# The order of the steps of a four-layer transformer kernel, written out step by step

## The chip, the cores and the metric

The kernel runs on one core of one Trainium2 chip. The metric is the device time of one execution in microseconds (us). Five queues of instructions run side by side: TensorE (PE; its weight loads are shown apart as PEld), VectorE (DVE), ScalarE (ACT), GpSimd (POOL) and SyncE (SP), which here issues all DMAs.

## What is computed

A batch of 4 items of 512 tokens by 256 channels goes through four blocks, all in float32:

```python
# layer 0: one head of 256; rmsnorm and film, q/k/v, softmax, projection, rmsnorm and film, MLP 256-1024-256
attn = softmax(einsum('bnd,bmd->bnm', Q, K) * D ** -0.5); x = x + (attn @ V @ proj_w + proj_b)
# layer 1: 16 heads of 16, modulated layernorm, q and k normalised to length one, gated residuals
q = l2norm(q) * exp(min(scale_mul, log 100)); k = l2norm(k); o = softmax(q @ k.T) @ v
# layer 2: 16 heads of 16, modulated layernorm, scale 16 ** -0.5, gated residuals
# layer 3: 16 heads of 16, attention and projection, then a modulated layernorm; no MLP
```

## The kernel before

**Work.** A job is one item in one layer: job j has layer j // 4 and item j % 4, 16 jobs in all. Jobs 0 to 3 have one head. Jobs 4 to 15 have 16 heads, in 4 units of 4 heads; unit u belongs to job u // 4. Most matrix products split each float32 operand in a high and a low part and add three products (`product`, lines 602 to 604).

**Steps.** The program is a list of 2446 steps, `PLAN`, each a triple (kind, job or unit or layer, index). Every engine walks through the whole list and issues its own part of each step, so the list alone sets the order on each of the five queues; between the queues there are semaphores, and each wait names the step that it waits for. Kinds that the text speaks of:

- `scores` (line 701): 16 steps a unit, one 64-row matmul each, for one head (n = i % 4) and one block of 128 keys; ScalarE then takes the exponential into `probs` (line 908, or line 905 for two neighbouring banks at once in layer 1).
- `max` (line 676): 16 steps a unit in layers 2 and 3, a 63-row matmul of the scores the other way round; VectorE reduces each to row maxima (line 1231). `shift` (line 693) transposes a unit's maxima, VectorE copies them to `cT` (line 1238), and SyncE writes them as the last row of the stack `SQ` (line 570) that `scores` of that unit read. In layer 1 a bound (`gmax`, line 684; `shift1`, line 689; `crow`, line 560) takes its place.
- `av` (line 714): the product of `probs` and the values, 4 steps a unit; the last is copied out by ScalarE.
- `hT1`, `hT2`, `q`, `k`, `v`, `qktok`, `oT1`, `oT2`, `proj`, `fc1`, `gelu`, `fc2a`, `fc2`: transposes, projections and MLP of a job. `gelu` is a step of ScalarE and GpSimd alone (lines 968 and 1334); `fc1`'s banks are read there. `stat1`, `norm1`, `stat2`, `norm2` are the layer norms. `modrow` and `mod` (lines 626 and 631) make a layer's modulation. `scores0`, `soft0`, `pT0` are the attention of layer 0.
- `load_*`, `split_*`: a piece of weights is loaded into one buffer and split into high and low part; a load waits until the piece before it is split. `stack`: six DMAs that build the stacks of one unit's q and k.

**Banks.** All matmuls but `av` write to one of `RING` = 7 banks, which are handed out in turn over the list (`USES`); `claim` makes TensorE wait until the step seven uses before it has been read:

```python
                n = USE[(kind, a, i)]
                if n >= RING:
                    k, b, m = USES[n - RING]
```

Scores and maxima of heads with even and odd n lie in different halves of the array's rows (`r = BLK * (n % 2)`). In layer 1 `double` finds the pairs of scores whose banks are neighbours:

```python
            return bounded(unit_job(a)) and USE[(kind, a, i - i % 2 + 1)] == first + 1 and first % RING < RING - 1
```

**The order before.** Each kind has a table of times in ticks (16 ticks a job), for the first jobs one table each, for the others one a layer; `multi_window` goes through a job in pairs of ticks, and a pattern such as "p6 A p8 0 p4 1" says how the 16 scores and maxima of a pair of ticks (p), the two `av` steps (A) and the remaining steps of each tick (0, 1) follow each other.

Of the kernel before, what the change touches and what calls it, by code (L numbers as in the profile page):

```python
# [61 lines left out]

SINGLE0 = {"stat1": (-16.2,), "norm1": (-23.7,), "hT1": (-15.4, -14.74), "q": (-11.01, -9.91), "k": (-5.2, -3.95),
           "v": (2.61, 5.47), "scores0": (-0.85, -0.65, 1.31, 3.06), "soft0": (1.31, 1.96, 4.26, 4.92),
           "pT0": (6.87, 7.42, 7.68, 9.03), "proj": (10.18, 10.73), "stat2": (13.99,),
           "norm2": (14.84,), "bias": (-3.15,)}
SINGLE1 = {"stat1": (-19.05,), "norm1": (-4.8,), "hT1": (-9.18, -8.83), "q": (-6.12, -4.01), "k": (-6.57, -5.31),
           "v": (2.6, 3.92), "scores0": (-1.64, -1.29, 1.78, 2.88), "soft0": (2.49, 2.84, 3.36, 3.71),
           "pT0": (7.11, 7.47, 7.82, 8.68), "proj": (11.73, 12.09), "stat2": (13.82,),
           "norm2": (14.33,), "bias": (-5.4,)}  # L70
SINGLE2 = {"stat1": (-16.5,), "norm1": (-14.55,), "hT1": (-9.7, -9.49), "q": (-6.76, -3.06), "k": (-5.65, -3.6),
           "v": (3.0, 4.07), "scores0": (-0.14, 0.81, 1.78, 4.23), "soft0": (2.59, 4.44, 5.01, 5.51),
           "pT0": (7.92, 8.38, 8.63, 8.99), "proj": (12.74, 12.9), "stat2": (16.24,),
           "norm2": (16.64,), "bias": (-0.3,)}
FFN0 = {"hT2": (16.72, 17.27), "fc1": (20.32, 20.68, 21.03, 21.44, 24.73, 25.09, 26.87, 27.22), "gelu": (21.79, 27.58),
        "fc2a": (24.96, 26.06), "fc2": (30.07, 32.88)}
# [1416 lines left out]
```

## Time and profile before

| | before |
|---|---|
| median of 3 runs | 1159.32 us (1157.16 to 1162.14) |
| profiled execution, its own time | 1158.51 us |
| its span, first to last instruction | 1156.7 us |
| mean granted TensorE clock | 0.985 of full speed |
| busy: PE, PEld, DVE, ACT, POOL | 94%, 61%, 61%, 69%, 42% of the span |

Times in the rows are from the start of the span. Layer 0 has TensorE to itself until about 225 us; the scores of layer 1 begin at 225.1 us, those of layer 2 at 550.6 us, those of layer 3 at 885.2 us. "A <- B" with a time is the time that A's engine sat idle until B released it. Matmuls are pipelined: a row's duration reaches past the start of the next, so the distance of starts is the rate.

### The profile page before, as it was taken

What the parts mean: (1) busy time and instruction counts of PE and PEld (TensorE: products, weight loads), DVE (VectorE), ACT (ScalarE), POOL (GpSimd) and SP (SyncE); (2) the same over time, 40 slices, a digit from 0 to 9 for tenths busy, and PEclk for the clock granted to TensorE, in tenths of its full rate; (3) what the DMA queues carried; (4) which work ended last, traced back from release to release, by engine and by line L of the source; (5) the groups of instructions that cost most, each with busy time, mean ns of one, the idle gap of its engine ahead of it and who ended that gap; (6) DMA issues with size and microseconds to landing.
All of it is one profiled execution on the core that took longest, in us unless ns stands there. A gap on an engine that the chain in (4) does not pass through costs nothing.

```text
span 1156.7 us, 19632 instructions
## 1 busy us (share of the span) xinstructions
PE 1085.3 (94%) x6697; PEld 706.0 (61%) x6697; DVE 702.5 (61%) x1479; ACT 794.0 (69%) x1331; POOL 490.3 (42%) x446
## 2 busy tenths in 40 slices
PE   8799989789899999999999999999999999999985
PEld 5577878555565656656657566666656566555442
DVE  6554446545264364234864865865865856898974
ACT  3563655477888678796686686687686787686763
POOL 2553642613633633654335453244344345254122
PEclk9999999999999999999999999999999999999998
DMA  7000001213303203221132231032121211232301
GB/s 234 18 29 28 1 20 38 52 31 101 88 28 95 54 2 90 75 64 29 28 84 65 69 102 38 2 83 65 41 71 29 52 42 52 55 84 56 84 12 36
DMA packets 36385, 64.45 MB, mean 56 GB/s; under 512 B 7208, under 2 KB 22312, under 8 KB 36288
## 3 DMA queue, kind: packets, MB, share of 16 engines
q1 hardware_dynamic: 36288, 63.20, 20.6%
q8 instruction: 56, 0.92, 0.3%
q14 instruction: 41, 0.34, 0.1%
HBM read 22.90 MB, written 2.12 MB: 22 GB/s over the span
## 4 chain that ended last, share of the span: by engine, by line
PE 72%; DVE 9%; ACT 8%; issue 5%; POOL 4%; DMA 1%; SPq 0%; POOLq 0%; DVEq 0%; ACTq 0%
PE AVB L714 13%; PE rings L602 13%; PE rings L604 11%; PE rings L603 11%; PE rings L701 10%; PE rings L676 6%; DVE m L1231 2%; ACT probs L908 2%; PE rings L754 2%; PE rings L749 2%; PE rings L645 2%; POOL gT_l L1334 1%; ACT L908 1%; PE rings L766 1%; POOL tok L1355 1%
## 5 line engine op out<-in xcount | busy, mean ns | idle before, releaser
L1231 DVE TENSOR_REDUCE m<-rings 128x1 fp32r<-128x512 f32 x512 | 319.1, 682 | 101.6 <-PE rings L676 78.4
L908 ACT ACTIVATE probs<-rings 128x512 f32<-128x512 f32 x570 | 297.3, 617 | 96.0 <-PE rings L676 84.5
L701 PE MATMUL rings<-SQ,SK 64*128 64x512 f32 x768 | 236.3, 440 | 12.5 <-ACT probs L905 4.7
L676 PE MATMUL rings<-SK,SQ 63*128 63x512 f32 x512 | 200.9, 459 | 5.4 <-ACT probs L908 4.2
L714 PE MATMUL AVB<-probs,V 128*32 128x512 f32 x1536 | 192.9, 609 | 0.6 <-issue 0.4
L701 PEld LDWEIGHTS rings<-SQ,SK 64*128 64x128 f32 x768 | 107.9, 185 | 139.1 <-issue 52.6
L1334 POOL TENSOR_TENSOR gT_l<-gT_f,gT_h 128x512 fp32r<-128x512 f32 x96 | 121.1, 1282 | 73.9 <-ACT gT_h L968 71.9
L905 ACT ACTIVATE probs<-rings 128x1024 f32<-128x1024 f32 x99 | 97.4, 1035 | 35.9 <-PE rings L701 21.9
L602 PE MATMUL rings<-w_h,gT_h 128*128 128x256 f32 x384 | 111.3, 290 | 2.8 <-POOL gT_l L1334 2.0
L676 PEld LDWEIGHTS rings<-SK,SQ 63*128 63x128 f32 x512 | 84.5, 185 | 39.6 <-ACT probs L908 33.0
L603 PE MATMUL rings<-w_l,gT_h 128*128 128x256 f32 x384 | 107.6, 280 | 0.0
L604 PE MATMUL rings<-w_h,gT_l 128*128 128x256 f32 x384 | 107.5, 280 | 0.0
L968 ACT ACTIVATE gT_f<-rings,colv 128x512 f32<-128x512 f32 x96 | 66.8, 696 | 30.1 <-PE rings L604 27.3
L714 PEld LDWEIGHTS AVB<-probs,V 128*32 128x32 f32 x1536 | 39.9, 110 | 75.8 <-issue 61.7
L602 PEld LDWEIGHTS rings<-w_h,gT_h 128*128 128x128 f32 x384 | 73.2, 191 | 14.1 <-issue 7.6
L602 PE MATMUL rings<-postT_h,w_h 128*128 128x512 f32 x192 | 78.2, 407 | 3.6 <-ACT gT_h L968 2.4
L1329 POOL TENSOR_TENSOR postT_l<-postT_f,postT_h 128x512 fp32r<-128x512 f32 x24 | 32.1, 1337 | 112.7 <-ACT postT_h L844 112.3
L1368 POOL TENSOR_TENSOR tmp<-tmp,gates 128x512 f32<-128x512 f32 x32 | 41.1, 1284 | 88.3 <-DVE tmp L1298 47.0
L604 PE MATMUL rings<-postT_h,w_l 128*128 128x512 f32 x192 | 75.4, 393 | 0.0
L603 PE MATMUL rings<-postT_l,w_h 128*128 128x512 f32 x192 | 75.3, 392 | 0.0
L1298 DVE TENSOR_TENSOR tmp<-rings,rowp 128x512 f32<-128x512 f32 x40 | 27.5, 688 | 78.4 <-PE rings L604 78.4
L1329 POOL TENSOR_TENSOR hT_l<-hT_f,hT_h 128x512 fp32r<-128x512 f32 x30 | 38.7, 1293 | 85.3 <-ACT hT_h L844 85.1
(190 smaller groups left out, 2188.6 us busy)
## 6 DMA issues: line engine op xcount, KB each, us to landing
SQ<-qh SPq DMA_DIRECT2D x96, 128.0 KB, 2.6
SK<-kh SPq DMA_DIRECT2D x96, 128.0 KB, 2.8
SQ<-ql SPq DMA_DIRECT2D x48, 128.0 KB, 2.7
SK<-kl SPq DMA_DIRECT2D x48, 128.0 KB, 2.9
raw<-in_w SPq DMA_DIRECT2D x20, 256.0 KB, 2.7
wmod_s<-in_wmod SPq DMA_DIRECT2D x6, 512.0 KB, 4.2
...
```

Of the source, the lines that this page charges most:

```text
L602: pe.matmul(out, sh, mh, start=first, stop=False)
L603: pe.matmul(out, sh, ml, start=False, stop=False)
L604: return pe.matmul(out, sl, mh, start=False, stop=last)
L676: mm = pe.matmul(o[:, :], SQ[a % 4][r:r + KS, n // 2, c * P:(c + 1) * P], SK[a % 4][r:r + KS, n // 2, :], start=True, stop=True)
L701: mm = pe.matmul(o[:, :], SK[a % 4][r:r + KS + 1, n // 2, c * P:(c + 1) * P], SQ[a % 4][r:r + KS + 1, n // 2, :], start=True, stop=True)
L714: mm = pe.matmul(AVB[32 * n:32 * n + 32, :], V[j % 2][:, i, (HD + 1) * h:(HD + 1) * h + 32], probs[:, (4 * t + n) % PROBS, :], start=(i == ...
L905: act.activation(probs[:, n % PROBS:n % PROBS + 2, :], two_banks(kind, a, i), ACT.Exp, scale=SCALE[layer(unit_job(a))]).then_inc(done["sco ...
L908: act.activation(probs[:, n % PROBS, :], bank(kind, a, i)[:, :], ACT.Exp, scale=SCALE[layer(unit_job(a))]).then_inc(done["scores"], 1)
L968: ins = act.activation(dst[:, m % (MT // 2), :], bank("fc1", a, m)[:, :], ACT.Gelu, bias=colv[:, layer(a), col:col + 1])
L1231: nc.vector.tensor_reduce(m16[:, col:col + 1], bank(kind, a, i)[:, :], AX_X, ALU.max, negate=True).then_inc(done["max"], 1)
L1329: nc.gpsimd.tensor_tensor(lo, full, hi.bitcast(F32), ALU.subtract).then_inc(done[kind], 1)
L1334: nc.gpsimd.tensor_tensor(gT_l[:, m, :], gT_f[:, m, :], gT_h[:, m, :].bitcast(F32), ALU.subtract).then_inc(g_lo, 1)
```

## The change

The tables and patterns go. A text, `TURNS`, names all steps in order by a code of one or two letters and a count ("s m2" is one `scores` and two `max`), 17 strings in all; `sequence` gives for each kind its steps in a fixed order, and `plan_steps` takes the next one of a kind for each code. The operations of a step and the waits between steps are made by the same code as before, from the new list. The diff, cut to its core:

```diff
--- before.py
+++ after.py
@@ -59,167 +59,113 @@
...
-LEAD_IN = {"stat1": (-24.09,), "norm1": (-23.23,), "hT1": (-14.74, -14.56), "qktok": (-12.53, -12.04, -11.51, -10.52),
-           "qkss": (-12.22, -11.69, -11.15, -10.36), "qkroot": (-10.28,), "v": (-7.19, -7.01), "qkrs": (-9.94,),
-           "qknorm": (-9.71, -9.63, -9.35, -9.17), "q": (-8.33, -7.97), "k": (-8.15, -7.79),
-           "stack": (-7.03, -6.95, -0.36, 1.0),
-           "gmax": (-5.39, -5.21, -5.03, -4.85, -4.67, -4.49, -3.6, -3.42, -2.52, -2.34, -2.16, -1.98, -1.8, -1.62, -1.44, -1.26),
-           "shift1": (-0.98, -0.98), "crow": (-0.9, 0.28, 1.7, 1.7)}
...
-PAIR = ("p6 A p6 0 p6 1", "p4 A p6 0 p4 1", "p8 A p2 0 p8 1", "p6 A p6 0 p6 1", "p6 A p8 0 p4 1", "p6 A p8 0 p6 1", "p6 A p8 0 p4 1", "p6 A p8 0 p4 1")
-PAIR_LAST = ("p10 A p6 0 p2 1", "p4 A p8 0 p4 1", "p6 a p6 0 p4 b p2 1", "p6 0 a p4 1 b", "p6 A p8 0 p4 1", "A p6 0 p6 1", "p8 a p8 0 p2 b p2 1", "p6 A 0 p8 1")
...
-def timed(table, j):
-
-    return [(TICKS * j + at, (kind, UNITS * j + i, 0) if kind in ("stack", "crow") else (kind, j, i))
-            for kind, times in table.items() for i, at in enumerate(times)]
-
-
-def around(j):
-
-    if not multi(j):
-        return [s for s in timed((SINGLE0, SINGLE1, SINGLE2, SINGLE3)[j], j) if s[1] not in FIRST] + timed((FFN0, FFN1, FFN2, FFN3)[j], j)
-    steps = timed(LEAD_IN, j) if j == BATCH else timed(COSINE if layer(j) == 1 else QKV if j > 2 * BATCH else {**QKV, **TO_LAYER2}, j)
-    if j == JOBS - 1:
-        return steps + timed(LAST, j)
-    return steps + timed(ATTN, j) + timed(FFN if layer(j) < LAYERS - 1 else OUTPUT, j)
-
-
-def layer_steps(l):
-
-    if l == 0:
-        return [(at, s) for table in (FIRST, NEXT1) for s, at in table.items()]
-    steps = []
-    for kind, times in (FOR_LAYER if l < LAYERS - 1 else FOR_LAST).items():
-        ahead = kind in ("load_mod", "modrow", "mod", "load_gate", "load_qkv", "split_qkv")
-        for i, at in enumerate(times):
-            if kind not in ("modrow", "mod", "load_mod") or i < mod_rows(l + 1):
-                steps.append((TICKS * BATCH * l + at, (kind, BATCH * l + i, 0) if kind in ("gatecast", "vones") else (kind, l + ahead, i)))
-    return steps
-
-
-def row_pairs(scores, maxima):
-
-    if not maxima:
-        return scores
-    return [s for n in (0, 2) for s in (scores[n], maxima[n + 1], scores[n + 1], maxima[n])]
-
-
-def in_order(pattern, pairs, av, rest):
-
-    out, n = [], 0
-    for what in pattern.split():
-        if what in "Aab":
-            out += av if what == "A" else av[:1] if what == "a" else av[1:]
-        elif what[0] == "p":
-            out += pairs[n:n + int(what[1:])]
-            n += int(what[1:])
-        else:
-            out += rest[int(what)]
-    return out + pairs[n:]
-
-
-def multi_window(w, work):
-
+CODE = {"s": "scores", "m": "max", "a": "av", "t": "shift", "g": "gmax", "u": "shift1", "K": "stack", "C":
+        "crow", "h": "hT1", "q": "q", "k": "k", "v": "v", "Q": "qktok", "Z": "qkss", "R": "qkroot", "I": "qkrs", "N":
+        "qknorm", "o": "oT1", "O": "oT2", "p": "proj", "b": "stat1", "n": "norm1", "B": "stat2", "M": "norm2", "H":
+        "hT2", "f": "fc1", "G": "gelu", "e": "fc2a", "d": "fc2", "r": "modrow", "c": "mod", "y": "gate", "Y": "gateout",
+        "X": "gatecast", "F": "gatefix", "lm": "load_mod", "lg": "load_gate", "lr": "load_rows", "lq": "load_qkv", "lp":
+        "load_wp", "lf": "load_w1", "ld": "load_w2", "wq": "split_qkv", "wp": "split_wp", "wf": "split_w1", "wd":
+        "split_w2", "V": "vones", "i": "bias", "S": "scores0", "z": "soft0", "P": "pT0", "E": "headscale", "L": "fold",
+        "T": "final", "W": "store", "A": "base", "D": "centre"}
+
+
+def sequence(kind):
+
+    jobs, ffn, many = range(JOBS), range(JOBS - BATCH), range(BATCH, JOBS)
+    units, layers, gated = range(UNITS * BATCH, UNITS * JOBS), range(LAYERS), range(1, LAYERS)
+    places = {"scores": (units, 16), "av": (units, TT), "stack": (units, 1), "shift": (units[UNITS * BATCH:], 2),
+              "crow": (units[:UNITS * BATCH], 1), "load_gate": (gated, 1), "gate": (gated, 1), "gateout": (gated, 1),
+              "gatecast": (many, 1), "oT1": (many, TT), "oT2": (many, CH), "hT2": (ffn, CH), "fc1": (ffn, MT),
+              "gelu": (ffn, 2), "fc2a": (ffn, 2), "fc2": (ffn, 2), "norm2": (jobs[:-1], 1), "fold": (range(1), 2),
+              "headscale": (range(1, 2), 1), "base": (jobs[-1:], 2), "centre": (jobs[-1:], TT), "load_rows": (layers, 1)}
+    if kind == "max":
+        return [(u, i ^ 1) for u in units[UNITS * BATCH:] for i in range(16)]
+    if kind in ("load_mod", "modrow", "mod"):
+        return [(l, i) for l in layers for i in range(mod_rows(l))]
+    if kind in ("load_w1", "load_qkv"):
+        first = (0, 2, 3, 1) if kind == "load_w1" else (0, 2, 1)
+        return [(l, i) for l in layers for i in (sorted(first) if l else first)]
+    if kind == "bias":
+        return [(j, 0) for j in (0, 1, 2, 3, 12, 13, 15, 14)]
+    if kind == "vones":
+        return [(j, 0) for l in (1, LAYERS - 1) for j in (BATCH * l, BATCH * l + 1)]
+    if kind in ("scores0", "soft0", "pT0"):
+        return [(j, t) for j in range(BATCH) for t in range(TT)]
+    if kind in ("qktok", "qkss", "qknorm"):
+        return [(j, t) for j in many[:BATCH] for t in range(TT)]
+    if kind in ("qkroot", "qkrs", "gmax", "shift1"):
+        return [(j, i) for j in many[:BATCH] for i in range({"gmax": 16, "shift1": 2}.get(kind, 1))]
+    if kind in ("final", "store", "gatefix"):
+        return [(j, i) for j in jobs[-BATCH:] for i in range(1 if kind == "gatefix" else TT)]
+    if kind.startswith(("load", "split")) and kind not in places:
+        return [(l, i) for l in layers for i in range({"qkv": 3, "wp": 1}.get(kind.split("_")[1], 4))]
+    there, n = places.get(kind, (jobs, 1 if kind in ("stat1", "norm1", "stat2") else 2))
+    return [(a, i) for a in there for i in range(n)]
+
+
+def mod_rows(l):
+
+    return 2 if l < LAYERS - 1 else 1
+
+
+TURNS = (
+    "b n lf r c wq h lm wq h b wq L q2 k lq k n lq lm L lq wp v",
+    "S2 z h lp z v h S lf wf2 S P wf z r wd z P k P lf ld E q lf P lr k c lm i q wf p i p B",
...
+    "s2 m s m a2 s m s m2 s o h o h o2 s m2 s a m s m s a t2 m s2 m3 O q O s3 m k p m s m s m s p s3 m3 a2 s m2 s2 "
+    "m B q k s2 t2 a s m2 s2 m a M s m s m s m v H m s m2 H a m s m s m s a m s m2 s2 v s3 m3 f G K c f3 m lq m2 t2 "
+    "b s a K a m wq s5 e m s2 m2 s e s K m2 s m s a2 m2 s lq s n m2 f4 G m s m2 t2 a m s a m K m2 s lg s m d s m s3",
+    "s d s lq s2 m3 a m s m s3 a X m s m3 s h o4 h a2 t2 s wq m3 s m V O lp O q k p s2 m s m2 p s2 m2 s m a s2 m2 s "
+    "m a s m2 s2 B wq m q k s2 t2 a m s3 M s2 a m4 s H v m s2 m s m2 K H a s2 m2 s2 a s b m s n m s m G f4 v m s t2 "
+    "a m s m s a m3 s m s e s2 m s m2 a2 s m2 s2 m e s2 m s m2 f4 G m2 t K m t s a2 s m3 s2 d s m s K m s2 h2 m2",
+    "s m d s X s m2 s m a2 s m s2 m s o4 s m s V m t a2 s2 m K m t O q O m2 s2 K k p m3 s3 p m s m s2 m a m s m s B "
+    "s2 a m3 s m s q k M v s2 t2 a s m2 s m2 H y H m s m s a s m s2 m s a m s m s3 a b m2 s G m f4 v n s m4 s e m "
...
+    "s2 m a m s3 m s o2 t o m s2 i W s m2 a o s t s2 m s m3 O2 a s2 F m4 p s m2 s K p m s m B s3 a s2 t a t m s3 m2 "
+    "s M a s2 m s2 m2 a T s m s m s m a s m2 s T s T m a m s X m s m s F s a s t s t W s5 W a s W s T s4 a s a A s6 "
+    "a s3 a3 o W o3 O2 p2 W B D2 W2 T W D2 T A T2",
+    )
+
+
+def plan_steps():
+
+    turn = {kind: iter(sequence(kind)) for kind in CODE.values()}
     plan = []
+    for token in " ".join(TURNS).split():
+        code = token.rstrip("0123456789")
+        for _ in range(int(token[len(code):] or 1)):
+            plan.append((CODE[code], *next(turn[CODE[code]])))
     return plan
```

## Rows read from the trace of the kernel before

**Rows 1.** The page, busy time, share of the span and instructions of each engine.
```profile
PE 1085.3 (94%) x6697; PEld 706.0 (61%) x6697; DVE 702.5 (61%) x1479; ACT 794.0 (69%) x1331; POOL 490.3 (42%) x446
```

**Rows 2.** Busy time by stretch: length, then each engine's busy us, granted clock, DMA.
```profile
core 0: us, PE busy (x) PEld busy (x) DVE busy (x) ACT busy (x) POOL busy (x), PEclk, DMA share, GB/s
...
550.60:885.20 334.60, 328.74 (x2094) 209.86 (x2090) 227.57 (x456) 247.87 (x439) 146.93 (x124) 1.00 0.22 57
...
968.00:1102.00 134.00, 131.80 (x848) 72.33 (x846) 119.04 (x240) 94.81 (x182) 48.65 (x56) 1.00 0.28 71
```

**Rows 3.** Timeline of TensorE, two runs in layer 2: start us, us, what.
```profile
657.43 0.50 PE L701 MATMUL rings<-SQ,SK 64*128 64x512 f32 x1
...
657.77 0.40 PE L701 MATMUL rings<-SQ,SK 64*128 64x512 f32 x1
...
658.01 0.40 PE L701 MATMUL rings<-SQ,SK 64*128 64x512 f32 x1
...
658.25 0.40 PE L701 MATMUL rings<-SQ,SK 64*128 64x512 f32 x1
...
659.14 0.50 PE L602 MATMUL rings<-hT_h,wqkv_h 128*128 128x512 f32 x1
...
665.70 0.39 PE L701 MATMUL rings<-SQ,SK 64*128 64x512 f32 x1
...
666.42 0.39 PE L701 MATMUL rings<-SQ,SK 64*128 64x512 f32 x1
...
666.91 0.39 PE L701 MATMUL rings<-SQ,SK 64*128 64x512 f32 x1
...
667.49 0.39 PE L602 MATMUL rings<-wqkv_h,hT_h 128*128 128x256 f32 x1
```

**Rows 4.** Waits of the weight loads, 550 to 885 us: total, times, longest.
```profile
PEld rings L676 <- ACT probs L908: 22.4, 62, 0.9
```

**Rows 5.** Waits of the weight loads, 885 us to the end.
```profile
PEld rings L701 <- DVE m L1231: 28.8, 56, 1.7
...
PEld rings L676 <- ACT probs L908: 9.8, 35, 0.5
```

**Rows 6.** Timeline of VectorE and ScalarE, readers back to back.
```profile
654.89 2.48 DVE L1231 TENSOR_REDUCE m<-rings 128x1 fp32r<-128x512 f32 x4
...
654.49 2.08 ACT L908 ACTIVATE probs<-rings 128x512 f32<-128x512 f32 x4
...
301.75 1.94 ACT L905 ACTIVATE probs<-rings 128x1024 f32<-128x1024 f32 x2
```

**Rows 7.** Timeline of TensorE, single waits ahead of layer 1; in brackets idle before.
```profile
37.87 0.32 PE L631 MATMUL rings<-unit,sq 4*128 4x4 f32 x3 [3.09 <-ACT sq L828]
...
57.95 0.47 PE L602 MATMUL rings<-kh,qh 128*128 128x512 f32 x1 [1.61 <-issue]
...
221.61 0.34 PE L689 MATMUL rings<-unit,m 64*64 64x64 f32 x2 [2.45 <-DVE m L1211]
```

**Rows 8.** Waits of the weight loads, 225 to 550 us.
```profile
PEld rings L701 <- ACT probs L905: 8.6, 11, 1.8
...
PEld rings L684 <- ACT probs L905: 5.1, 7, 0.9
```

**Rows 9.** Groups by line and shape: busy us, mean ns of one, idle before.
```profile
L968 ACT ACTIVATE gT_f<-rings,colv 128x512 f32<-128x512 f32 x96 | 66.8, 696 | 30.1 <-PE rings L604 27.3
...
L968 ACT ACT_TABLE_LOAD x21 | 26.9, 1283 | 3.3 <-PE rings L604 3.0
```

**Rows 10.** Timeline of TensorE and SyncE, the path of a shift row.
```profile
662.68 0.43 PE L693 MATMUL rings<-unit,m 64*16 64x64 f32 x2
...
665.15 1.30 SPq L570 DMA_DIRECT2D SQ<-cT  x2
...
222.35 1.45 SPq L560 DMA_DIRECT2D SQ<-cT  x2
...
225.08 0.72 PE L701 MATMUL rings<-SQ,SK 64*128 64x512 f32 x4 [0.18 <-DMA SQ<-cT]
```

More of the change, by code:

```diff
@@ L59, in direct @@
     return layer(j) in (0, LAYERS - 1)
[L63 to L76, printed above, removed]
@@ L98 @@
-QKV = {"hT1": (-18.7, -14.34), "q": (-12.95, -10.7), "k": (-12.7, -10.05), "v": (-8.75, -5.2),
-       "stack": (-8.25, -7.85, -2.25, 0.45), "stat1": (-22.35,), "norm1": (-20.3,)}
-ATTN = {"oT1": (17.1, 17.56, 17.57, 17.83), "oT2": (18.45, 18.71), "proj": (19.2, 19.85), "stat2": (20.7,),
-        "norm2": (22.55,)}
-FFN = {"hT2": (23.5, 23.91), "fc1": (25.6, 25.81, 25.82, 25.83, 29.55, 29.56, 29.57, 29.58), "gelu": (25.84, 29.59),
-       "fc2a": (27.45, 29.55), "fc2": (30.55, 31.2)}
-FFN3 = {"hT2": (23.3, 23.76), "fc1": (25.6, 25.61, 25.72, 25.73, 29.65, 29.66, 29.67, 29.68), "gelu": (25.74, 29.69),
-        "fc2a": (26.65, 27.9), "fc2": (31.15, 31.55)}
@@ L186, in multi_window @@
-def multi_window(w, work):
-    plan = []
-    for t in range(0, TICKS, 2):
-        pairs, rest = [], []
-        for x in (t, t + 1):
-            g, c = divmod(x, TT)
-            v = x + LEAD
-            u = UNITS * w + v // TT
-            pairs += row_pairs([("scores", UNITS * w + g, 4 * c + n) for n in range(4)],
-                               [("max", u, 4 * (v % TT) + n) for n in range(4)] if u < UNITS * JOBS and not bounded(u // UNITS) else [])
-            if v % TT == 0 and u - 1 < UNITS * JOBS and not bounded((u - 1) // UNITS):
-                pairs[len(pairs) - SHIFT_BACK:len(pairs) - SHIFT_BACK] = [("shift", u - 1, 0), ("shift", u - 1, 1)]
-            now = [s for at, s in work if x <= at - TICKS * w < x + 1]
-            pairs += [s for s in now if s[0] in ("gmax", "shift1")]
-            rest.append([s for s in now if s[0] not in ("gmax", "shift1")])
-        n = TICKS * w + t
-        av = [("av", x // TT, x % TT) for x in (n - 2, n - 1)] if n > TICKS * BATCH else []
-        plan += in_order((PAIR7 if w == 2 * BATCH - 1 else (PAIR, PAIR1, PAIR, PAIR_LAST)[layer(w)])[t // 2], pairs, av, rest)
-    return plan
+CODE = {"s": "scores", "m": "max", "a": "av", "t": "shift", "g": "gmax", "u": "shift1", "K": "stack", "C":
[7 rows of a table added]
@@ L208, in mod_rows @@
 def mod_rows(l):
     return 2 if l < LAYERS - 1 else 1
-def plan_steps():
-    work = [s for j in range(JOBS) for s in around(j)] + [s for l in range(LAYERS) for s in layer_steps(l)]
-    work = sorted(s for s in work if s[1] not in START)
-    plan = START + [s for at, s in work if at < TICKS * BATCH]
-    for w in range(BATCH, JOBS):
-        plan += multi_window(w, work)
-    plan += [("av", UNITS * JOBS - 1, n) for n in (TT - 2, TT - 1)]
-    return plan + [s for at, s in work if at >= TICKS * JOBS]
+TURNS = (
[45 rows of a table added]
+    )
```

40 lines of the change are left out of this document (2 added, 38 removed), and 35 rows, old and new, of tables (FIRST, TURNS).

## The prediction

> **What bounds the kernel now.** I read the page's busy shares first, then the busy time by stage, then the starts of single matmuls, and last who the weight loads waited for. The busy share of TensorE is 94% [rows 1], and in layer 2 of the model (550.6 to 885.2 us) it is 328.74 of 334.60 us [rows 2]. Taken at its word that leaves nothing to gain. The starts say otherwise. Scores and maxima are issued in pairs that use different halves of the array's rows, and in one stretch the scores start at 657.77, 658.01 and 658.25: a pair every 0.24 us. The fourth pair of that run holds the engine until 659.14, which is 0.89 us, and all of it counts as busy. In the next run the fourth, fifth and sixth pair take 0.72, 0.49 and 0.58 us [rows 3]. So "busy" hides waiting: 0.65, 0.48, 0.25 and 0.34 us over the free rate, 0.43 on average.
>
> What they wait for is a bank. Seven banks are handed out in turn; a score's bank comes free when ScalarE has taken the exponential, a maximum's when VectorE has reduced it. From 550 to 885 us the weight loads of the maxima wait 22.4 us for exponentials [rows 4]; from 885 us on the loads of the scores wait 28.8 us for maxima and those of the maxima 9.8 us for exponentials [rows 5]. Back to back the readers need 2.48 / 4 = 0.62 us for a maximum and 2.08 / 4 = 0.52 us for an exponential [rows 6], so a pair costs the readers 0.62 us (they work side by side) against 0.24 us of TensorE. Three pairs fit into seven banks at the free rate; from the fourth on TensorE goes at the readers' pace. Yet the readers are not full over the stage: VectorE works 227.57 and ScalarE 247.87 of 334.60 us in layer 2. In the last layer this holds less: VectorE works 119.04 of 134.00 us from 968 to 1102 us [rows 2].
>
> In the name of the Trainium skill (Trainium Kernel Development and Optimization, Performance Expectations): matmul busy time is a bad measure, since matmuls are pipelined. The starts above agree: 94% busy and 0.43 us lost in a pair.
>
> **The change, part by part.** I wrote out both orders. Both have the same 2446 steps, so no work is removed; only the sequence on each queue differs, and with it which bank a step gets. The counts that follow are of steps in the two orders.
>
> *Long runs.* Before there are 203 runs of scores and maxima without another TensorE step between; 63 of them have more than 7 members, and 153 pairs stand beyond the third of their run (6 in layer 1, 62 in layer 2, 85 in the last). After there are 269 runs, 3 with more than 7 members, and 23 pairs beyond the third (2, 4, 17). That takes 4, 58 and 68 pairs out of the slow place, at 0.43 us each 1.7, 24.9 and 29.2 us. Bounds: nothing, if the wait only moves to the next run's first pair, and all 55.8 us. In layer 2 VectorE and ScalarE have a quarter of the stage free, but not evenly, so I keep two thirds, 16.6 us. In the last layer VectorE's own work is the cover: from 968 to 1102 us there are only 134.00 - 119.04 = 15 us to win, of which I take 11, and 4 around it. Sum: -33.3 us.
>
> *Switches.* The steps that cut the runs cost something. The first pair of a run takes 657.77 - 657.43 = 0.34 us instead of 0.24 [rows 3]: 0.10 us when TensorE goes from one kind of step to another. Such switches rise from 680 to 793: 3 in layer 1, 10 ahead of it, 48 in layer 2, 52 in the last. At 0.10 us that is 11.3 us; in the last layer half lies under VectorE's work. I take +8.7 us; bounds 0 and 11.3.
>
> *Pairs taken apart.* Before, no score or maximum stands alone; after, 58 do (26, 11, 21), because the new runs have odd lengths. Two lone ones need two slots where a pair needs one: 29 slots of 0.24 us, 7.0 us. In layer 2 I count all (1.3), elsewhere half, since a reader is nearer to full: +4.1 us; bounds 0 and 7.0.
>
> *ScalarE.* In layer 1 two scores in neighbouring banks share one exponential: 1.94 / 2 = 0.97 us against 2 x 0.52 [rows 6]. 99 pairs do so before and 88 after, as more of them are separated: 11 x 0.07 = 0.8 us. Going through ScalarE's order gives 52 changes between exponential, GELU and root instead of 50; a table load takes 1.283 us [rows 9], so 2.6 us. Half of the 3.4 us is on the path: +1.7 us; bounds 0 and 3.4.
>
> *Single waits ahead of layer 1.* The second modulation waited 3.09 us for ScalarE's copy of its row; after, six steps stand between. The scores of the second item waited 1.61 us behind their own q; after, two output projections are between. The bound of the fifth item (L689) waited 2.45 us for maxima; after, three fc1 steps are between [rows 7]. Each filler is longer than the wait: -7.1 us; the bounds are 0 and that.
>
> *Layer 1.* Weight loads wait 8.6 and 5.1 us for the two-bank exponentials [rows 8]. Counting TensorE's work between the release of a bank and its next claim, 25 scores of this layer have under 0.7 us before and none after. I take half of the 13.7 us, -6.9 us; bounds 0 and all.
>
> *DMA queue.* SyncE issues its DMAs in the order of the steps. The first 14 keep their places; later, weight loads move past stacks and shifts by a few places, and a load that waits for the buffer holds the stack behind it. In the two later layers an item's first stack has at least 10.7 us of TensorE work ahead of its use after the change against 9.2 before, so I cost this at nothing; the cover gone, it would be one wait of a few us.
>
> Sum: -33.3 + 8.7 + 4.1 + 1.7 - 7.1 - 6.9 = -32.8 us. The profiled execution took 1158.51 us (0.8 below the median of the runs shown): 1158.5 - 32.8 = 1126 us.
>
> The Trainium skill (TensorE: Matmul & The Clock Gate, Step-by-step: what each phase is for) says that TensorE pulls weight loads ahead of matmuls still running. By that a switch of kind would be free and the sum 1126 - 8.7 = 1117 us; the trace shows 0.10 us, since a step's wait stands in front of its load, and I go by the trace.
>
> **The rivals.** *The readers are the limit* (slower). Cutting a run doesn't make VectorE and ScalarE faster; if they have a backlog where the runs are, each wait moves to the first pair of the next run, and the switches and lone matmuls come on top: +11.3 + 7.0 + 3.4 - 7.1 = +14.6, 1173 us. For it: VectorE at 89% late in the last layer. Against it: 68% and 74% in layer 2. It decides where a reader is above some nine tenths over the stage, which one stretch of 134 us is.
>
> *TensorE is the limit* (no change). If its busy time is real, the most that layer 2 and the last can give is idle time, 334.60 - 328.74 = 5.9 and 134.00 - 131.80 = 2.2 us [rows 2]. With the waits of layers 0 and 1: -8.1 - 7.1 - 6.9 + 21.7 = -0.4, 1158 us. Against it are the starts above.
>
> *Late producers* (half the gain). Some distances shrink. A shift matmul at 662.68 has its row issued at 665.15 [rows 10], and an issue at 222.35 let TensorE go on at 225.08, 2.7 us later: 5.2 us in all. In layer 2 no unit has under 5.8 us of TensorE work there before; after, three have 3.8 to 4.8. GELU needs 1.283 + 8 x 0.696 = 6.9 us [rows 9] before GpSimd's share; from its first fc1 to fc2a there stood 9.8 us in layer 2, and after the change 6.4 to 9.4. If 16 such places in layers 1 and 2 lose 1 us each, 1126 + 16 = 1142 us.
>
> **How the numbers follow.** Chances: the forecast 0.66, late producers 0.13, TensorE the limit 0.10, readers the limit 0.11. The forecast's own range is 1095 to 1137: below, all of the weight loads' waits go, 22.4 + 28.8 + 9.8 + 13.7 = 74.7, and 7.1, against 21.7 of costs, -60.1 or 1098 us, rounded down; above, two fifths of the runs' 55.8 us go instead of three fifths, 1126 + 11. To leave no more than 2 in 10 out, the range reaches past the late producers, to 1155, and leaves out the two upper cases. About 0.5%, 5.8 us, is what a measurement of this kernel can tell from no change. Faster: 0.66 + 0.13 + a little of the third, 0.80; within: 0.09; slower: 0.11.
>
> **What would show it.** Right: runs of scores and maxima whose pairs all start 0.24 to 0.34 us apart; the weight loads' waits for exponentials and maxima after 550 us at half or less of 61 us; layer 2 shorter by 10 to 15 us with VectorE's and ScalarE's busy time as before, so higher shares; no wait of 3 us before the second modulation; 88 two-bank exponentials. Wrong: first pairs of runs that take 0.6 us and more, or score loads that wait for the shift rows' DMA.

## The result and the profile after

The new order takes 1064.82 us (median; 1063.27 to 1067.09) against 1159.81 us (1157.16 to 1162.14) of the order before, run beside it: a ratio of 0.9183, with an interval of 0.9156 to 0.9210. That is 95 us less, where 33 were forecast and 60 was the most that the forecast's own range had reckoned with.

Lines of the code stand 54 lower in the profile after (the scores' L701 is L647, the maxima's L676 is L622, `av` L660, the products L548 to L550); in the experiments a few lines lower still. First the page's busy times and its chain of waits, which for the kernel before began "PE 72%; DVE 9%; ACT 8%; issue 5%":

```profile
PE 1030.9 (97%) x6697; PEld 676.1 (64%) x6697; DVE 717.8 (68%) x1479; ACT 796.9 (75%) x1344; POOL 490.7 (46%) x446
...
PE 83%; DVE 7%; ACT 3%; issue 2%; POOL 2%; DMA 1%; SPq 1%; POOLq 0%; DVEq 0%; ACTq 0%
```

TensorE's idle time was 1156.7 - 1085.3 = 71.4 us and is 1062.3 - 1030.9 = 31.4; its busy time fell by 54 us, although not one matmul is gone. VectorE and ScalarE work about as long as before, 15 us (2%) and 3 us longer [rows 1]. Where it went is read from busy time by stage. The stages are cut at the first score of layers 1, 2 and 3 and of the last unit, so that each holds some steps of its neighbours; the stage called layer 0 has the first bounds of layer 1 in it [rows 7]. The kernel before, its first four stages:

```profile
0.00:225.10 225.10, 199.66 (x1073) 160.93 (x1073) 125.95 (x314) 107.92 (x189) 99.42 (x96) 0.98 0.17 50
225.10:550.60 325.50, 303.06 (x1928) 192.93 (x1930) 143.20 (x285) 254.63 (x361) 144.93 (x121) 0.98 0.23 62
...
885.20:1126.50 241.30, 235.68 (x1495) 133.27 (x1494) 193.85 (x393) 171.48 (x320) 90.57 (x96) 0.99 0.21 53
```

(layer 2 is in [rows 2]), and the kernel after:

```profile
0.00:202.50 202.50, 194.00 (x1077) 161.07 (x1077) 134.65 (x314) 111.57 (x192) 103.61 (x98) 0.99 0.18 54
202.50:498.00 295.50, 288.57 (x1925) 187.12 (x1924) 150.95 (x287) 253.75 (x373) 142.83 (x120) 0.99 0.25 64
498.00:808.50 310.50, 308.78 (x2080) 195.00 (x2076) 225.50 (x455) 245.25 (x436) 142.76 (x123) 1.00 0.25 65
808.50:1034.20 225.70, 223.60 (x1514) 124.52 (x1511) 194.76 (x393) 175.39 (x325) 96.62 (x103) 1.00 0.23 60
```

Layer 0 is 22.6 us shorter, layer 1 30.0, layer 2 24.1, layer 3 15.6, the tail 2.1. The forecast, shared out the same way, had about 6, 5, 10.5 and 11. So more than half of the gain, and two thirds of the miss, lie ahead of layer 2, where the forecast had hardly looked.

The runs look as forecast. TensorE in layer 2, single `av` between short runs:

```profile
595.34 0.72 PE L622 MATMUL rings<-SK,SQ 63*128 63x512 f32 x3
595.68 0.61 PE L647 MATMUL rings<-SQ,SK 64*128 64x512 f32 x2
595.92 0.40 PE L622 MATMUL rings<-SK,SQ 63*128 63x512 f32 x1
596.24 1.07 PE L660 MATMUL AVB<-probs,V 128*32 128x512 f32 x8
597.24 0.50 PE L647 MATMUL rings<-SQ,SK 64*128 64x512 f32 x2
597.58 0.41 PE L622 MATMUL rings<-SK,SQ 63*128 63x512 f32 x2
597.91 1.07 PE L660 MATMUL AVB<-probs,V 128*32 128x512 f32 x8
```

First pairs take 0.34 us (595.34 to 595.68), the next one 0.24; no pair of these rows waits. Waits of the weight loads, from 498 to 808.5 us and from there to the end, beside [rows 4, 5]:

```profile
PEld rings L622 <- ACT probs L854: 4.9, 8, 1.3
PEld rings L647 <- DVE m L1177: 4.5, 7, 0.8
...
PEld rings L622 <- DVE m L1177: 3.4, 4, 0.8
...
PEld rings L647 <- ACT probs L854: 3.2, 5, 0.8
```

```profile
PEld rings L622 <- DVE m L1177: 13.2, 22, 0.8
...
PEld rings L647 <- DVE m L1177: 9.8, 15, 0.8
PEld rings L647 <- ACT probs L854: 9.1, 13, 2.1
...
PEld rings L622 <- ACT probs L854: 3.2, 6, 0.8
```

The three waits that the prediction named, 22.4, 28.8 and 9.8 us, are 4.9, 9.8 and 3.2. But scores and maxima no longer stand in fixed pairs, and other combinations have come up: with all of them the sum falls only from 72.6 to 51.3 us. A load's wait is not yet a wait of TensorE: part of it lies under the `av` that still runs. In layer 1 the loads of the scores wait 2.9 us for two-bank exponentials instead of 8.6 [rows 8].

**A count over the whole kernel.** For each step of TensorE I took the distance to the next step's start and subtracted the shortest distance that this kind of step shows. The sums, "excess" from here on, are waits, switches and slow clock together; beside them is what ScalarE did during the parts over 0.2 us.

| us | layer 0 | layer 1 | layer 2 | layer 3 |
|---|---|---|---|---|
| excess before | 45.8 | 73.8 | 68.0 | 62.7 |
| excess after | 22.9 | 43.2 | 44.6 | 43.3 |
| over 0.2 us, ScalarE in exponentials, before / after | 3.2 / 0.2 | 26.9 / 11.3 | 34.6 / 4.7 | 34.4 / 12.0 |
| ScalarE in other copies, GELU or a table load, before / after | 19.4 / 6.2 | 19.7 / 4.6 | 8.9 / 4.3 | 2.3 / 1.3 |

With the tail the excess falls from 258 to 159 us, about the whole gain. By what ScalarE did meanwhile, it is waits for banks that went in layers 2 and 3, waits behind ScalarE's other work in layer 0, and both in layer 1; the experiments test this.

### The profile page after: what moved, and what is told of

It is laid out like the page before. It is cut to its first block, busy times and chain, and to the rows that moved or that the text cites. A ratio compares the mean times of both kernels' runs of the same rounds, so it can differ in the third digit from the quotient of the medians.

```text
span 1062.3 us, 19653 instructions
## 1 busy us (share of the span) xinstructions
PE 1030.9 (97%) x6697; PEld 676.1 (64%) x6697; DVE 717.8 (68%) x1479; ACT 796.9 (75%) x1344; POOL 490.7 (46%) x446
## 3 DMA queue, kind: packets, MB, share of 16 engines
q1 hardware_dynamic: 36288, 63.20, 22.4%
## 4 chain that ended last, share of the span: by engine, by line
PE 83%; DVE 7%; ACT 3%; issue 2%; POOL 2%; DMA 1%; SPq 1%; POOLq 0%; DVEq 0%; ACTq 0%
PE AVB L660 15%; PE rings L548 15%; PE rings L550 13%; PE rings L549 13%; PE rings L647 10%; PE rings L622 6%; PE rings L591 2%; DVE m L1177 2%; PE rings L695 2%; PE rings L700 2%; POOL gT_l L1280 1%; PE rings L572 1%; PE rings L712 1%; ACT gT_h L914 1%; ACT gT_f L914 1%
## 5 line engine op out<-in xcount | busy, mean ns | idle before, releaser
L854 ACT ACTIVATE probs<-rings 128x512 f32<-128x512 f32 x592 | 315.5, 612 | 92.8 <-PE rings L647 63.1
L647 PE MATMUL rings<-SQ,SK 64*128 64x512 f32 x768 | 199.8, 439 | 2.2 <-DMA SQ<-cT 1.2
L660 PE MATMUL AVB<-probs,V 128*32 128x512 f32 x1536 | 198.9, 603 | 1.5 <-issue 1.5
L622 PE MATMUL rings<-SK,SQ 63*128 63x512 f32 x512 | 149.9, 437 | 1.2 <-ACT probs L854 0.4
L647 PEld LDWEIGHTS rings<-SQ,SK 64*128 64x128 f32 x768 | 92.7, 185 | 86.3 <-issue 38.4
L548 PE MATMUL rings<-w_h,gT_h 128*128 128x256 f32 x384 | 111.7, 291 | 1.9 <-DVE modb L977 1.2
L550 PE MATMUL rings<-w_h,gT_l 128*128 128x256 f32 x384 | 106.6, 278 | 0.0
L622 PEld LDWEIGHTS rings<-SK,SQ 63*128 63x128 f32 x512 | 69.8, 185 | 54.3 <-issue 16.9
L851 ACT ACTIVATE probs<-rings 128x1024 f32<-128x1024 f32 x88 | 87.2, 1042 | 11.0 <-PE rings L647 5.2
L660 PEld LDWEIGHTS AVB<-probs,V 128*32 128x32 f32 x1536 | 36.4, 108 | 74.6 <-issue 58.3
L548 PEld LDWEIGHTS rings<-w_h,gT_h 128*128 128x128 f32 x384 | 72.1, 188 | 17.6 <-issue 4.0
L548 PE MATMUL rings<-postT_h,w_h 128*128 128x512 f32 x192 | 78.1, 407 | 0.0
L550 PE MATMUL rings<-postT_h,w_l 128*128 128x512 f32 x192 | 75.5, 393 | 0.0
L549 PEld LDWEIGHTS rings<-w_l,gT_h 128*128 128x128 f32 x384 | 72.3, 188 | 0.2
L550 PEld LDWEIGHTS rings<-w_h,gT_l 128*128 128x128 f32 x384 | 72.2, 188 | 0.0
L1242 DVE TENSOR_TENSOR tmp<-rings,tmp 128x512 f32<-128x512 f32 x24 | 16.5, 688 | 76.0 <-PE rings L550 76.0
```

The lines of the kernel that those rows point to most:

```text
L548: pe.matmul(out, sh, mh, start=first, stop=False)
L549: pe.matmul(out, sh, ml, start=False, stop=False)
L550: return pe.matmul(out, sl, mh, start=False, stop=last)
L622: mm = pe.matmul(o[:, :], SQ[a % 4][r:r + KS, n // 2, c * P:(c + 1) * P], SK[a % 4][r:r + KS, n // 2, :], start=True, stop=True)
L647: mm = pe.matmul(o[:, :], SK[a % 4][r:r + KS + 1, n // 2, c * P:(c + 1) * P], SQ[a % 4][r:r + KS + 1, n // 2, :], start=True, stop=True)
L660: mm = pe.matmul(AVB[32 * n:32 * n + 32, :], V[j % 2][:, i, (HD + 1) * h:(HD + 1) * h + 32], probs[:, (4 * t + n) % PROBS, :], start=(i == ...
```

## The experiments

Steps are written kind.job.index or kind.unit.index. A pair "beyond the third" is one of a run of scores and maxima with three pairs ahead of it in the run. Layer 0 has one and the same order in the kernel before and in four of the experiments, and its end then lay between 225.1 and 228.1 us; a difference of 3 us in one profile is no effect. What an experiment costs against the full change is the difference of the two medians, which were taken at different times; by the ratios to the kernel before, which was run beside each, it comes out up to 1.8 us different.

**Cutting the runs of the old order by its patterns (short_runs).**

```diff
-PAIR = ("p6 A p6 0 p6 1", "p4 A p6 0 p4 1", ...)
-PAIR_LAST = ("p10 A p6 0 p2 1", ...)
+PAIR = ("a p6 0 b p6 1 p4", "a p4 0 p4 b p4 1 p4") * 4
+PAIR_LAST = ("a p6 0 b p6 1 p4", "a p4 0 p4 b p4 1 p4") * 4
```

> Only the eight patterns of layers 2 and 3 are changed in the old order; all tables, and the order of every other kind, stay. Pairs beyond the third of their run fall from 62 to 0 in layer 2 and from 85 to 21 in layer 3 (the full change: 4 and 17); switches rise from 680 to 804; no score or maximum stands alone. Theory 'banks' (a pair beyond the third waits for a reader): 126 such pairs x 0.2 to 0.3 us net of switches = 25 to 38 us, layer 2 shorter by 15 to 20 and layer 3 by about 10, 1120 to 1135 us. Rival 'other moves' (layers 2 and 3 gained 24 and 16 us because the projections, transposes and MLP steps stand elsewhere, the runs only look better): within 10 us of before, 1150 us or more.

Measured: 1184.9 us, a ratio of 1.0205 (1.0175 to 1.0235): about 2% slower. Both theories missed. Layer 2 took 349.4 us for 334.6. During TensorE's waits there ScalarE was in exponentials for 21.0 us instead of 34.6, so the banks did come free, but it was idle for 14.2 instead of 3.7: other producers were late. One of them, in the timeline of TensorE, is a shift row that the pattern had put too close to its scores:

```profile
682.86 0.76 PE L701 MATMUL rings<-SQ,SK 64*128 64x512 f32 x1 [4.07 <-DMA SQ<-cT]
```

**Filling single waits in the old order (singles).** Sixteen places; one of them:

```diff
-av.17.0 scores.17.10 .11 .12 .13 q.5.0 k.5.0 hT2.3.0 q.5.1 gate.1.0 hT2.3.1 k.5.1 av.17.1 scores.17.14
+av.17.0 scores.17.10 .11 hT2.3.0 hT2.3.1 scores.17.12 .13 av.17.1 q.5.0 k.5.0 q.5.1 gate.1.0 k.5.1 scores.17.14
```

> Only sixteen places of layers 0 and 1 are changed in the old order: at each, a step at which TensorE waited 1 to 3.4 us in the profile before is put behind one to four steps that were ready. The excess over the free rate at these places sums to 30.5 us. Theory 'single waits' (layers 0 and 1 lost their time at few places, and a wait costs a stretch at a lower granted clock besides): 20 to 35 us faster, 1125 to 1140 us, and no stretch of layer 0 or 1 under 0.85 of the clock except the first. Rival 'bound elsewhere' (ScalarE's exponentials and GELU set the pace of layer 1, so a wait taken away appears again at the next step): under 10 us, 1150 us or more.

Measured: 1176.56 us, 1.0130 (1.0100 to 1.0160): slower, 16 us in layer 1 alone. The fillers weren't ready. At the place shown TensorE still waits 1.28 us, now for `hT2.3.0`. The like place of the next item (`hT2.4.0`) fared worse; TensorE's timeline and the stretches there:

```profile
348.43 1.94 PE L584 MATMUL rings<-unit,tok 128*128 128x128 f32 x8 [3.84 <-DVE tok L1069]
```

```profile
345.00:350.00 5.00, 1.57 (x8) 1.57 (x8) 3.29 (x8) 3.44 (x7) 0.00 (x0) 0.73 0.00 0
350.00:355.00 5.00, 5.00 (x26) 2.60 (x25) 0.33 (x1) 4.21 (x7) 2.54 (x2) 0.59 0.00 0
```

The transposes `hT2` had stood behind q because their norm isn't done earlier. The wait of 1 us at this second place became one of 3.84, and behind it the granted clock was 0.59. The run tells that these moves were badly chosen; it doesn't tell what single waits cost.

**Both edits together (both).**

> The edits of the two kernels above together. If runs and single waits are separate causes, the two savings add: before minus the sum of the two, 1090 to 1110 us, within 4 us of the sum. If one pace limits both, clearly less than the sum. What is left to the full change (1065 us) is then what neither explains: the runs of layer 1, and the smaller waits.

Measured: 1199.53 us, 1.0334 (1.0300 to 1.0368): the two losses, 2.05% and 1.30%, add. The signs were wrong, the independence right.

**The new order up to layer 2, the old one behind (new_to_l2).**

> The new order up to the first score of layer 2, the old one from there on. The profiles of before and after put the first score of layer 2 at 550.6 and at 498.0 us. Theory 'stages add': 1159 - 53 = 1106 us, layers 2 and 3 as long as before. Rival 'given back': the layers behind wait for what the early part has pushed (weights, stacks), and more than 10 us of the 53 are lost again, over 1116 us.

Measured: 1105.59 us, 0.9517 (0.9484 to 0.9550). The first score of layer 2 starts at 499.6 us, and layers 2 and 3 take 334.1 and 241.0 us, as before. The stages add; nothing is given back, and 56 of the 95 us come from ahead of layer 2.

**Single moves into the long runs of the old order (cut_runs).**

```diff
-fc1.8.3 ... shift.39.1 av.38.0 av.38.1 scores.38.10 max.40.3 scores.38.11 max.40.2 scores.38.12 ...
+fc1.8.3 ... shift.39.1 av.38.0 scores.38.10 max.40.3 scores.38.11 max.40.2 av.38.1 scores.38.12 ...
```

> The old order with 48 single steps of layers 2 and 3 (37 av, 8 projections, 2 v, 1 fc2), each moved later into the middle of the long run behind it, past at most six scores and maxima; no step is moved earlier than another kind's work it might still wait for. Pairs beyond the third of their run fall from 62 to 2 in layer 2 and from 85 to 51 in layer 3, claims of a bank with under 0.7 us of work since its last use from 91 to 3 and from 142 to 83; switches rise by 83. Theory 'banks, if nothing else comes late': layer 2 shorter by 12 to 20 us, layer 3 by 4 to 10, 1134 to 1144 us. Rival 'the waits only move' (as the kernel with the short patterns suggests, which was slower): layer 2 within 4 us of its 334.6, 1155 us or more.

Measured: 1172.97 us, 1.0100 (1.0073 to 1.0128). Neither theory had a loss. The shown place is one of eight that are alike. ScalarE and TensorE in the kernel before, then with the moves:

```profile
684.24 1.28 ACT L908 ACT_TABLE_LOAD   x1
685.54 3.05 ACT L908 ACTIVATE probs<-rings 128x512 f32<-128x512 f32 x6
...
686.19 0.49 PE L676 MATMUL rings<-SK,SQ 63*128 63x512 f32 x1 [0.58 <-ACT probs L908]
```

```profile
689.52 1.28 ACT L848 ACT_TABLE_LOAD   x1
690.81 2.07 ACT L848 ACTIVATE probs<-rings 128x512 f32<-128x512 f32 x4
...
691.46 0.50 PE L616 MATMUL rings<-SK,SQ 63*128 63x512 f32 x1 [1.42 <-ACT probs L848]
```

ScalarE is in GELU and loads its table back; no exponential comes before that ends. Before, both `av` (0.88 us each) lay under this; now one does, TensorE waits longer by the other's 0.84 us, and the other is still to be done. By the starts of equal steps in the two traces, the stretches from the eight places took 13.9 us more, those from the other forty 5.2 us less.

**The same moves without the eight (cut_clean), and the eight alone (uncover8).**

> The kernel with the 48 moved steps again, but eight av of layer 2 (the second av of units 34, 35, 38, 39, 42, 43, 46, 47) stay where the old order has them: TensorE works on them while ScalarE takes GELU and loads its table back. In the trace with all 48 moves the stretches from these eight places were 1.1 to 2.8 us longer than before (13.9 us in all), the other forty together 5.2 us shorter. Theory 'cover' (an av moved behind the wait that it covered is paid in full): 1152 to 1158 us, a little under before. Rival 'the cuts themselves lose' (83 more switches of kind at 0.10 us): 1164 us or more.

> The old order with only those eight av moved, by four scores and maxima each. Eight matrix products of 0.88 us change places, nothing else. Theory 'cover': 8 x 0.8 to 1.2 us and, where the wait grows to 2 us, a stretch at a lower granted clock: 8 to 15 us slower, 1168 to 1176 us. Rival: within 4 us of before.

Measured: cut_clean 1155.06 us, 0.9968 (0.9954 to 0.9982); uncover8 1177.48 us, 1.0163 (1.0139 to 1.0187). "Cover" holds in both. Eight moved products cost 2.3 us each in the median, more than expected; layer 2, where they stand, takes 348.2 us in the profile, 1.7 more for each. But cut_clean also shows that 86 pairs taken out of the slow place (153 to 67 over all layers) are worth 3.7 us in the old order, not 86 x 0.43 = 37. The likely reason is that a single `av` put into a run had to come out of the work just ahead of it, where the readers were catching up; the count at the end of this section shows where the waits went.

**The runs undone in the new order (long_again).** At 35 places of layers 2 and 3:

```diff
-max.40.4 scores.38.15 fc2a.8.0 scores.39.0 max.40.7 scores.39.1 max.40.6 max.40.9 max.40.8 av.38.2
+max.40.4 scores.38.15 scores.39.0 max.40.7 scores.39.1 max.40.6 max.40.9 max.40.8 fc2a.8.0 av.38.2
```

> The new order with one thing undone: at 35 places of layers 2 and 3 the step or steps between two runs of scores and maxima (fc2a, fc2, projections, v, transposes; no av) are put behind the second run, so that the two runs become one. Each of these steps moves by less than 2 us; all else keeps its place. Pairs beyond the third rise from 23 to 113, claims with under 0.7 us from 13 to 153 in layers 2 and 3; switches fall by 43. Theory 'banks': 90 pairs x 0.43 = 38 us, less 4 us of switches, and less what overlaps: 20 to 35 us slower than the full change, 1085 to 1100 us. Rival 'runs don't matter' (the gain is in steps that no longer come too early): within 6 us of 1065.

Measured: 1109.08 us, 0.9550 of the kernel before (0.9524 to 0.9575) and 44.3 us slower than the full change. Layer 2 takes 336.3 us and layer 3 242.8, so that these 35 places give back 25.8 and 17.1 us, all that the change had won there (24.1 and 15.6). The stages of layers 2 and 3, and waits of the weight loads in layer 2:

```profile
499.50:835.80 336.30, 325.88 (x2078) 203.28 (x2076) 225.48 (x455) 245.12 (x437) 141.57 (x122) 0.98 0.23 60
835.80:1078.60 242.80, 235.30 (x1514) 130.89 (x1511) 194.84 (x393) 174.72 (x324) 97.54 (x104) 0.99 0.21 55
```

```profile
PEld rings L638 <- ACT probs L845: 12.1, 20, 2.1
PEld rings L638 <- DVE m L1168: 10.2, 18, 1.8
PEld rings L613 <- DVE m L1168: 8.3, 16, 1.1
PEld rings L613 <- ACT probs L845: 7.6, 20, 1.3
```

They sum to 38.2 us, against 4.9 + 4.5 + 3.4 + 3.2 = 16.0 after. During TensorE's waits ScalarE was in exponentials for 28.6 us (after 4.7, before 34.6). 44.3 / 90 is 0.49 us a pair. Not all of it is banks: at 637 us a pair waited 1.85 us for a shift row, and the stretches at a lower granted clock lose 10.2 us in place of 3.4 (below).

**The same with `av` alone (long_av).** At 26 places of the new order:

```diff
-scores.37.0 max.38.13 av.36.2 scores.37.1 scores.37.2 max.38.12 max.38.15 av.36.3
+scores.37.0 max.38.13 scores.37.1 scores.37.2 max.38.12 max.38.15 av.36.2 av.36.3
```

> The new order with 26 places of layers 2 and 3 undone, this time places where only av (27 of them, 0.88 us each) stand between two runs: they are put behind the second run. Pairs beyond the third rise from 23 to 93, nearly as in the kernel where the long steps were moved (113, which cost 44 us); switches fall by 36. Theory 'each pair beyond the third has its price' (0.43 to 0.49 us): 70 x 0.45 = 31, less 4, 1085 to 1095 us. Rival 'only the work that stood between counts' (a place can't lose more than the 0.88 us that was moved out of it, and where other work follows soon the readers catch up): 26 x 0.2 to 0.5 = 5 to 13 us, 1070 to 1078 us.

Measured: 1085.71 us, 0.9371 (0.9343 to 0.9399), 20.9 us slower than the full change. By its time it stands at the lower edge of the first theory. But the price of a pair is 20.9 / 70 = 0.30 us, not 0.45; per place it is 0.80 us, nine tenths of the 0.88 us that was moved out. Read so, a place lost what its run waits, but no more than what stood between. That is no general bound: the eight `av` of uncover8, as long, lost 1.7 us each.

**Runs undone in layer 1 (long_l1).** At eight places of the new order:

```diff
-gmax.6.12 scores.22.11 fc2a.4.0 scores.22.12 gmax.6.13 ... scores.22.15 fc2a.4.1
+gmax.6.12 scores.22.11 ... fc2a.4.0 scores.22.12 gmax.6.13 ... scores.22.15 scores.23.0 ... scores.23.4 fc2a.4.1
```

> The new order with eight places of layer 1 undone in the same way: the steps between two runs of scores and bound matmuls (three fc2a, two groups with fc2, one v, three av; 22.6 us of work in all) are put behind the second run. Pairs beyond the third, bound matmuls counted as members, rise from 4 to 24 in layer 1 (the old order has 21), claims of a bank with under 0.7 us of work from 0 to 24 (the old order: 25). Theory 'runs, in layer 1 too' (a pair there takes ScalarE about 1.0 us and TensorE 0.24): 20 pairs x 0.45 to 0.75 = 9 to 15 us slower than the full change, 1074 to 1080 us. Rival 'layer 1 gained 30 us by single waits alone': under 4 us, below 1069.

Measured: 1077.61 us, 0.9288 (0.9251 to 0.9324), 12.8 us slower than the full change, as the first theory had it; layer 1 alone takes 311.7 us in the profile, 16.2 more. I had not seen these runs: only when the bound matmuls (`gmax`) are counted as members does the old order have 21 pairs beyond the third in layer 1. The forecast had counted 6.

**Single waits put back in the new order (sites_back).** Six places; one of them:

```diff
-gmax.4.15 fc1.2.4 fc1.2.5 fc1.2.6 shift1.4.0 shift1.4.1 fc1.2.7
+gmax.4.15 shift1.4.0 shift1.4.1 fc1.2.4 fc1.2.5 fc1.2.6 fc1.2.7
```

> The new order with six places of layers 0 and 1 put back next to what they wait for, as the old order had them: the second modulation behind k of item 1, the first scores of item 3 directly behind k, the bound's transpose directly behind the sixteen bound matmuls, fc2a of item 2 two pairs earlier, q and k of the second item directly behind the norms, q and k of the third two pairs and two av earlier. The waits there in the profile before were 1 to 3 us each. Theory 'single waits add up': 9 to 13 us of waits and some us of lower granted clock behind them, 1074 to 1082 us. Rival 'slack' (later steps take the time back, the stages being held by ScalarE): under 4 us, below 1069.

Measured: 1081.77 us, 0.9318 (0.9287 to 0.9348), 17.0 us slower than the full change, as the theory of single waits had it. Layer 0 takes 216.2 us (13.7 more) and layer 1 302.3 (6.8 more); layers 2 and 3 are as after. The place in the diff, in TensorE's timeline, and the stretches there:

```profile
205.59 0.41 PE L627 MATMUL rings<-unit,m 64*64 64x64 f32 x2 [3.77 <-DVE m L1149]
```

```profile
200.00:205.00 5.00, 1.72 (x8) 0.66 (x6) 5.00 (x11) 0.00 (x0) 4.17 (x5) 1.00 0.00 0
205.00:210.00 5.00, 4.41 (x12) 3.50 (x13) 2.98 (x8) 1.05 (x2) 2.68 (x2) 0.51 0.17 34
210.00:215.00 5.00, 5.00 (x23) 4.15 (x22) 0.00 (x0) 3.26 (x6) 3.11 (x3) 0.81 0.80 224
```

TensorE stood idle for most of 200 to 205 us, and then went on at 0.51 of full speed, about the lower of its two levels, 1.2 GHz. The products of one kind behind the wait start 0.43 us apart and, once the clock is back, 0.23:

```profile
207.38 0.63 PE L540 MATMUL rings<-postT_h,w_h 128*128 128x512 f32 x1
207.80 0.63 PE L541 MATMUL rings<-postT_l,w_h 128*128 128x512 f32 x1
...
212.23 0.39 PE L540 MATMUL rings<-postT_h,w_h 128*128 128x512 f32 x1
212.46 0.39 PE L541 MATMUL rings<-postT_l,w_h 128*128 128x512 f32 x1
```

The 14 products from 205.93 to 212.00 us take 6.07 us instead of 14 x 0.23 = 3.2: this wait is paid a second time.

**An attempt at more (tuned).** 28 lone scores and maxima of layers 2 and 3 put in pairs again, and four waits of the new order filled, such as

```diff
-scores.30.10 fc2a.6.0 max.32.2 max.32.5 scores.30.11 scores.30.12 max.32.4
+scores.30.10 max.32.2 max.32.5 scores.30.11 scores.30.12 fc2a.6.0 max.32.4
```

> The new order with 30 lone scores and maxima of layers 2 and 3 moved by a few places so that they stand in pairs again (32 lone ones there become 4), and with four of its remaining waits filled: v of item 1 ahead of the first projection (1.6 us), v of job 4 ahead of its q (1.2), q of job 7 behind two more pairs of scores (2.2), fc2a of job 6 behind two more scores (1.4). Theory: 14 slots x 0.24 = 3.4 us from the pairs and 4 to 6 us from the waits: 1056 to 1060 us. Rival 'lone matmuls are hidden and the waits move on': within 3 us of 1065.

Measured: 1065.27 us, 0.9171 (0.9149 to 0.9194): no change. Layers 2 and 3 take 309.6 and 225.8 us (310.5 and 225.7). Pairing the lone matmuls gained nothing that can be told from noise. The wait at the place in the diff, which lies ahead of 498 us, only moved: 1.4 us ahead of `fc2a.6.0` became 1.4 us ahead of `max.32.2`. Behind it the granted clock was 0.76 and 0.56 (465 to 475 us; 1.00 in the full change), and `fc2a.6.0` took 5.42 us instead of 2.93, so what the other filled waits gained may be hidden by this. No kernel tried beats the change.

**The same excess by place in the run.** The count of the section on the result can be sorted by where a pair stands in its run of scores and maxima (a lone one counts as a pair). Layers 2 and 3 together, from the starts of the matmuls in the traces:

| us | before | after | long_again | long_av | cut_clean | short_runs |
|---|---|---|---|---|---|---|
| behind the third pair | 58.3 | 6.8 | 50.0 | 32.1 | 22.8 | 9.7 |
| first three pairs | 40.1 | 45.9 | 39.9 | 40.4 | 65.4 | 93.7 |
| other steps | 32.1 | 36.2 | 42.5 | 37.5 | 36.9 | 49.9 |

Before, 143 pairs stand behind the third there and lose 0.41 us each, close to the 0.43 of the prediction. The full change takes away 51.5 us of that, and 9.9 come back elsewhere. Cutting the old order takes away 35.5 us (cut_clean) and 48.6 us (short_runs), but 30.1 and 71.4 us come back, most of it at the first three pairs of a run: there the waits did move on. In layer 1, bound matmuls counted, the three rows are 11.4, 36.8 and 25.5 us before and 1.0, 19.0 and 23.9 after: the larger part of its loss had stood ahead of the fourth pair.

## Why the prediction was wrong

The sign and the mechanism of the runs were right, and so were most of the signs named: runs at 0.24 to 0.34 us a pair, the three waits named for banks at 17.9 of 61 us (though 51.3 of 72.6 with all combinations), 88 two-bank exponentials, VectorE and ScalarE as busy as before in a shorter layer 2. But that layer became 24.1 us shorter, not 10 to 15. The size of the whole was wrong by a factor of nearly three, and the range missed. By its steps:

- **Single waits ahead of layer 1, -7.1 us: far too small.** It priced three rows of [rows 7] that it had picked, as if they were all. Layer 0 became 22.6 us shorter. Its waits over 0.9 us sum to 30.3 us before (14 places) and 15.1 after. Putting four places of layer 0 back cost 13.7 us there.
- **Layer 1, -6.9 us: the step that failed most.** It took half of the two rows of [rows 8]. The layer became 30.0 us shorter. Missing were the runs with bound matmuls (eight places put back: 12.8 us) and the waits behind ScalarE's other work, 19.7 us before and 4.6 after (two places put back: 6.8 us). ScalarE works 254.63 and 253.75 us in it; its idle time fell from 70.9 to 41.8 us, by as much as the layer.
- **Long runs, -33.3 us: right mechanism and right price, too much held back.** It kept 31.6 of 54.1 us for layers 2 and 3. Sorted by place, 51.5 us went there and 9.9 came back elsewhere; putting back 35 places cost 44.3 us. The discount failed in layer 2, where it kept two thirds of 24.9 us: the loss behind the third pair fell from 26.5 to 0.8 us. In the last layer its bound held. Between the same two maxima (968.6 to 1101.8 us before, 888.5 to 1008.5 after) 133.2 us became 120.0, with VectorE busy for 89% and then 96%: 13.2 of the 15 us that it saw there, where it had taken 11.
- **Clock: no term.** Summed over stretches of 5 us, (1 - granted clock) x 5 us is 10.2 us before, 3.4 after, 15.3 in sites_back and 28.8 in singles. This sum is an estimate of what the lower level costs. Such stretches follow waits, so some waits were worth more than their own length (sites_back: 2.9 us on top of 3.77).
- **Lone matmuls, +4.1 us:** nothing measured (tuned). **Switches, +8.7 us:** the 0.10 us is there again in the first pairs above; the 9.9 us that came back in layers 2 and 3 hold it, but don't tell it from new waits. The Trainium skill (TensorE: Matmul & The Clock Gate, Step-by-step: what each phase is for) says that weight loads are pulled ahead of running matmuls when the row groups don't conflict or a background buffer takes them. The prediction left that condition out and read from it that a switch would be free; the trace has 0.34 against 0.24 us again. That the wait in front of the load is the reason, as the prediction says, no run shows. **ScalarE, +1.7 us:** its work rose by 2.9 us, as counted. **DMA queue, 0:** nothing in the profile after speaks against it.
- **The rivals.** "The readers are the limit" was wrong for the change, but right for a cut made within the old order: there the waits moved on, as it said (cut_runs, cut_clean). "TensorE is the limit" fell with layer 2. "Late producers" came with the new order only as one wait of 1.2 us for a shift row; they came in short_runs and singles, where steps were moved ahead of what they need.

The root is mostly one. The prediction took the named rows of the trace for the whole: its terms touch some 82 us of waits (61 + 13.7 + 7.1), and the excess was 258. The prediction said itself that "busy" hides waiting, and then summed only the waiting that the views name, less a discount in layer 2 for which it had no row. Its lower bound, all of the named waits, could not hold a change that moves every step.

What a pair is worth in a whole kernel is no constant either. In the new order 90 pairs more cost 0.49 us each (35 places with 2.2 us of work between on average, 77.8 us in all), 70 pairs 0.30 each (0.88 us between); in the old order 86 pairs fewer gave 0.04 each. At the place itself the price hardly differs: 0.41 us in the kernel before, and 35.5 / 86 = 0.41 for those that cut_clean took away. What differs is how much of it comes back elsewhere. The likely reading, argued from uncover8 and cut_clean: a run is worth cutting with work that is taken from where it covers nothing, and the old order had put it where it covered GELU and the readers' catching up.

**What stays open.** The three sets of places put back account for 13.7 us of layer 0's 22.6, for 6.8 and 12.8 (16.2 in the profile) of layer 1's 30.0, and for all of layers 2 and 3; they were run apart, not together. The rest of layers 0 and 1, 16 to 19 us, was not undone place by place, and its cause stays open. Whether the new places of the scores and maxima alone would do, with all other kinds in the old sequence, was not tried.
